# The bias of X's projection in a graph attention stage: from two VectorE additions a graph to one-row matmuls on TensorE, with the result copied out by ScalarE

## The reference, cut to what matters

```python
X = _heads(lrelu(node_feats @ W_lin + b_lin), B, N)      # lrelu(z) = leaky_relu(z, 0.01)
q = _heads(lrelu(node_feats @ W_q), B, N)
k = _heads(lrelu(node_feats @ W_k), B, N)
att = jax.nn.sigmoid(jnp.einsum('bhxd,bhyd->bhxy', q, k) * scale)
adj_h = adj_matrix[:, None] * att
deg = jnp.sum(adj_h, axis=-1)
dis = jnp.where(deg > 0, deg ** (-0.5), 0.0)
A = dis[..., :, None] * adj_h * dis[..., None, :]
Y = jnp.einsum('bhxy,bhyd->bhxd', A, X)
```

## Time and profile before

| | us |
|---|---|
| median of 3 runs (lowest to highest) | 1422.14 (1418.39 to 1423.32) |
| profiled execution | 1419.9 |
| span of its trace | 1418.2 |
| TensorE busy in the span | 1337.5 (94%) |
| VectorE busy | 962.3 (68%) |
| ScalarE busy | 794.9 (56%) |

### The profile page before, as it was taken

One profiled execution on the slowest core, in us unless ns is written; L12 is line 12 of the kernel. 1 busy time (PEld: TensorE's weight loads), 2 busy tenths in 40 slices (PEclk: granted clock), 3 DMA queues, 4 the chain that ended last, 5 costly groups with the idle time before them and its releaser, 6 DMA issues. The chain is left out here.

```text
span 1418.2 us, 27578 instructions
## 1 busy us (share of the span) xinstructions
PE 1337.5 (94%) x10184; PEld 806.0 (57%) x10184; DVE 962.3 (68%) x2147; ACT 794.9 (56%) x1334; POOL 581.7 (41%) x504
## 2 busy tenths in 40 slices
PE   5999999999999999986899999999999789999798
PEld 3455555668999999862233233333332467774498
DVE  2467887643343434357989999999996799856533
ACT  2466654644444444436676776777874578873300
POOL 2026777672545555301212132131143699972300
PEclk9999999999999999999999999999999999999999
DMA  9757757355888878555424534333331421004034
GB/s 312 274 178 251 288 161 236 118 179 149 248 252 240 253 242 252 173 153 178 142 90 135 162 102 126 93 118 108 102 105 45 117 61 46 16 1 98 1 107 134
DMA packets 200152, 214.37 MB, mean 151 GB/s; under 512 B 22949, under 2 KB 156645, under 8 KB 200020
## 3 DMA queue, kind: packets, MB, share of 16 engines
q1 hardware_dynamic: 191604, 195.24, 45.2%
q0 software_dynamic: 8416, 17.38, 3.4%
HBM read 170.51 MB, written 42.06 MB: 150 GB/s over the span
## 5 line engine op out<-in xcount | busy, mean ns | idle before, releaser
L1552 ACT ACTIVATE c_AH<-c_S 128x2048 f32<-128x2048 f32 x128 | 240.6, 1880 | 130.1 <-PE c_S L1417 129.8
L1586 DVE TENSOR_TENSOR c_AH<-c_AH,c_A 128x2048 f32<-128x2048 f32 x128 | 291.9, 2285 | 23.7 <-ACT c_AH L1552 16.3
L875 ACT ACTIVATE a_A<-a_DG,a_A 128x256 f32<-128x256 f32 (+2 forms) x202 | 94.8, 509 | 192.8 <-PE a_DG L728 191.7
L618 POOL DMA_INDIRECT ys<-a_A,a_targets x135 | 131.2, 972 | 142.3 <-DVE a_A L1090 123.8
L1375 POOL TENSOR_TENSOR c_raw<-c_deg,c_power 128x16 f32<-128x16 f32 x16 | 58.2, 3636 | 243.6 <-DVE c_deg L1643 243.6
L592 POOL DMA_INDIRECT rows<-a_S,a_slots x128 | 131.9, 1030 | 51.5 <-issue 51.5
L1444 PE MATMUL c_DG<-c_AH,c_ones 128*32 128x512 f32 x1024 | 137.3, 608 | 7.9 <-DVE c_AH L1586 7.9
L1417 PE MATMUL c_S<-c_Q,c_K 32*128 32x512 f32 x928 | 132.3, 640 | 5.1 <-ACT c_AH L1552 3.1
L1430 PE MATMUL c_YA<-c_AH,c_XT 128*32 128x512 f32 x1024 | 131.9, 593 | 0.3 <-DVE c_XT L1653 0.3
L698 PE MATMUL a_AG<-a_A,x 128*128 128x512 f32 x256 | 114.4, 595 | 0.0
L728 PE MATMUL a_DG<-a_A 128*128 128x256 f32 (+2 forms) x356 | 100.5, 406 | 1.2 <-DMA a_A<-xT_all 1.1
(11 more groups left out here) (428 smaller groups left out, 2497.7 us busy)
## 6 DMA issues: line engine op xcount, KB each, us to landing
a_A<-in_dram SPq DMA_DIRECT2D x76, 578.0 KB, 5.1
a_A<-in_dram SPq DMA_DIRECT2D x32, 1024.0 KB, 9.8
c_A<-in_dram SPq DMA_DIRECT2D x128, 256.0 KB, 2.6
a_A<-rows SPq DMA_DIRECT2D x60, 130.0 KB
G<-ys SPq DMA_DIRECT2D x10, 512.0 KB, 5.1
a_X<-in_dram SPq DMA_DIRECT2D x8, 512.0 KB, 13.4
a_R<-in_dram SPq DMA_DIRECT2D x8, 512.0 KB, 5.0
stream<-a_R SPq DMA_DIRECT2D x8, 512.0 KB, 9.7
```

The source lines that it names most:

```text
L618: pool.indirect_dma_start(ys, bass.IndirectOffsetOnAxis(ap=targets[g % NY][:, t:t + 1], axis=0), Y[g % NY][:, t, :], None, bounds_check=ys ...
L875: act.activation(hT[g % 2][:, f, 0:size(g)], up_bank(g, f)[:, 0:size(g)], ACT.Gelu, bias=w_of(g)[:, F_N + f:F_N + f + 1]).then_inc(h_ready, 1)
L1552: act.activation(AH[g % UNITS][:, :, :], S[:, :, :], ACT.Sigmoid, scale=HD ** -0.5).then_inc(att_ready, 1)
L1586: dve.tensor_tensor(ah[:, :, :], ah[:, :, :], A[g % ADJ_BUFS][:, :].unsqueeze(1).to_broadcast([P, HEADS, HALF]), ALU.mult).then_inc(ah_dve, 1)
```

## The change

`add_bias` and its two VectorE instructions a graph go. On TensorE each block of 128 nodes gets four more matmuls behind its four: the stationary operand is one row of 32 ones (`ones[0:1, :]`), the moving operand one row with the bias (`bias[0:1, :]`), and they accumulate onto the same four strips of `M`. On ScalarE a plain copy (`copy_X`) of `M` into `XR` stands behind the sigmoids of steps 6 and 7. The wait for the bias's load moves from VectorE to TensorE, that for the last graph's `XR` from VectorE to ScalarE.

```diff
                 elif what[:-1] == "x":
+                    if i == 0:
+                        pe.wait_ge(w_loaded, 48)
                     for c in range(*part):
                         for j in range(HEADS):
                             at = (4 * half + c) * P + j * HD
-                            mm = pe.matmul(M[quad(j), c * P:(c + 1) * P], xnT[:, at:at + HD], W[:, 2, :], start=True, stop=True)
+                            pe.matmul(M[quad(j), c * P:(c + 1) * P], xnT[:, at:at + HD], W[:, 2, :], start=True, stop=False)
+                        for j in range(HEADS):
+                            mm = pe.matmul(M[quad(j), c * P:(c + 1) * P], ones[0:1, :], bias[0:1, :], start=False, stop=True)
...
+            def copy_X(i, half):
+                act.wait_ge(side_full, full[f"x{half}", i])
+                wait(act, xs_ready, 2 * i)
+                act.activation(flat(XR[:, tiles(half), :]), M[:, :], ACT.Copy).then_inc(side_free, 1)
...
+                    if n in (6, 7) and is_graph(i):
+                        copy_X(i, n - 6)
...
-            def add_bias(i, half):
-                if i == 0:
-                    dve.wait_ge(w_loaded, 48)
-                dve.wait_ge(side_full, full[f"x{half}", i])
-                wait(dve, xs_ready, 2 * i)
-                dve.tensor_tensor(XR[:, tiles(half), :], quarter(M[:, :]), bias[:, :].unsqueeze(1).to_broadcast([P, 4, D]),
-                                  ALU.add).then_inc(side_free, 1)
...
-                    if n in (6, 7) and is_graph(i):
-                        add_bias(i, n - 6)
```

## The result

| | before | after |
|---|---|---|
| median of 4 runs (lowest to highest), us | 1421.59 (1418.39 to 1423.32) | 1453.21 (1448.08 to 1453.59) |
| profiled execution, us | 1419.9 | 1453.56 |
| span of its trace, us | 1418.2 | 1451.8 |

The changed kernel takes 1.0219 times as long, with a 95% interval of 1.0201 to 1.0236: 2.2% slower, 31.6 us between the medians. The forecast was 1452.0 us.

What follows compares the result with a forecast made beforehand. TensorE's list, without gaps from the second graph on, was taken to bound the attention stage. Seven graphs at 27.9 us, plus 3.3 for the first, less 0.5 for VectorE, gave +30.7 us: 1452 us, range 1440 to 1459.

Steps and rivals of the forecast that it cites:

- What bounds the kernel: Attention stage, second graph on: TensorE's list without idle time sets the 54.94 us period, VectorE does not.
- The streaming: TensorE's added bias matmuls: 0.218 us for each of 8 blocks, 1.74 us a graph, one contraction row no shorter than 128.
- The change of shape: TensorE alternating between 128*32 projection and 32*32 bias matmuls: 16 changes of 0.14 us, 2.24 us a graph.
- Rival B: TensorE switches from 128*32 to 32*32 at no price: 1.74 us a graph, period 56.7 us, 1435 us; chance 9%.
- The first graph: First graph of the stage: 3.98 us, less waits filled, plus half-clock cost, taken as 3.3 us, ends 0 to 5.0.
- the late half of C: ScalarE's copy makes the sigmoid late, TensorE idling before step 9's scores: 1457 us; C as a whole 7%.
- the waits of 0.51 and 0.22 us: First graph, steps 7 and 8: TensorE waits for ScalarE's sigmoid; added work can fall into these waits.
- the first job at half the clock: First graph, the job at 659 us: runs at granted clock 0.50 and may cost up to 1 us more.
- VectorE's gain: Eighth graph, step 10: losing the additions removes TensorE's 0.51 us wait for VectorE, a gain of 0.5 us.
- ScalarE: Copies in steps 6 and 7 stay off the path; the sigmoid of step 8 still waits 0.4 us for the scores.
- The sum: Whole kernel: 27.9 + 3.3 - 0.5 = +30.7 us, forecast 1452 us.

Runs made afterwards that it cites:

- experiment 1: Changed kernel without the one-row matmuls, so the bias is not added, ScalarE's copies kept: 1419.00 us against 1419.22 for the kernel before, ratio 0.9999.
- experiment 2: Changed kernel with VectorE instead of ScalarE copying M out at steps 6 and 7, one-row matmuls kept: 1451.78 us, ratio 1.0225 to the kernel before.
- experiment 7: Kernel before with VectorE's bias step split into an in-place addition and a separate copy out: 1421.53 us against 1419.95, ratio 1.0015.
- experiment 3: Changed kernel with bias matmuls of 128 contraction rows, in the projection's own array shape: 1432.33 us, ratio 1.0100 to the kernel before.
- experiment 6: Kernel of experiment 5 with its one-row matmul standing twice in each job, with ones of 0.5: 1455.73 us, ratio 1.0258 to the kernel before.
- experiment 4: Changed kernel with four 512-column one-row matmuls ahead of each job's projection, 4 shape changes a graph instead of 16: 1438.84 us, ratio 1.0139 to the kernel before.
- experiment 5: Changed kernel with one 512-column one-row matmul a job behind the scores, x0 whole behind step 6's degrees: 1438.73 us, ratio 1.0135 to the kernel before.

## Why the prediction was right, point by point

**What bounds the kernel: right.** TensorE's list set the period before (54.94 us), and does after. Experiments 1, 2 and 7 show it from three sides.

**The streaming: right.** 1.74 us a graph forecast, 1.75 measured (experiment 3). That one contraction row is as dear as 128 was read from the scores and the degrees, and holds: 512 columns of one row take 0.85 us (experiment 6), `x1`'s 512 columns of 128 rows 0.87.

**The change of shape: right, a little too high.** 0.14 us a change was taken from a block between two other shapes; experiments 3 and 4 give 0.135 and 0.13. For 16 changes that is 2.16 instead of 2.24 us, and the graph 3.91 instead of 3.98. Rival B, a period of 56.7 us, is the kernel of experiment 3 and not this one. So going from 128\*32 to 32\*32, with the column strips unchanged, pays like the pairs seen before. The Trainium skill's rule that a change of tiling mode drains TensorE ("TensorEngine Tiling (Array Packing)", "Tiling Modes") now has a price for this pair too, 0.13 to 0.135 us; the drain itself no row shows.

**The first graph: too low.** 3.3 us forecast, with 5.0 as the upper end; 4.6 measured. The rows of TensorE's first graph after, answering to the earlier trace rows:

```profile
658.69 1.93 PE L1444 MATMUL c_DG<-c_AH,c_ones 128*32 128x512 f32 x8 [4.99 <-DVE c_AH L1597]
660.40 0.66 PE L1479 MATMUL c_M<-W,xnT 128*32 128x128 f32 x8
...
662.73 2.09 PE L1417 MATMUL c_S<-carry,c_K 32*128 32x512 f32 x8
664.75 1.57 PE L1444 MATMUL c_DG<-c_AH,c_ones 128*32 128x512 f32 x8
666.15 0.39 PE L1479 MATMUL c_M<-W,xnT 128*32 128x128 f32 x8
...
667.53 1.14 PE L1417 MATMUL c_S<-carry,c_K 32*128 32x512 f32 x8
...
672.29 1.14 PE L1417 MATMUL c_S<-c_Q,carry 32*128 32x512 f32 x8
...
675.98 1.14 PE L1417 MATMUL c_S<-c_Q,carry 32*128 32x512 f32 x8 [0.97 <-ACT c_AH L1561]
```

From the first projection (660.40) on, the distances between it and the scores are 2.33, 4.80, 4.76 and 3.69 us; between the starts in the earlier trace rows (659.12, 660.13, 664.22, 667.45, 670.58) they are 1.01, 4.09, 3.23 and 3.13. The differences, 1.32, 0.71, 1.53 and 0.56, make 4.12; the other 0.5 us lies ahead of that, in steps that the change does not touch. Two things of it were not in my sum. The waits of 0.51 and 0.22 us were filled as forecast, but the one of 0.41 grew to 0.97: ScalarE's copy and normalisations stand ahead of the sigmoid, and in the first graph no products cover them. In experiment 2, without that copy, the row reads

```profile
672.99 1.14 PE L1417 MATMUL c_S<-c_Q,carry 32*128 32x512 f32 x8 [0.42 <-ACT c_AH L1561]
```

Idle time ahead of the scores of step 9 is the sign that the prediction gave for the late half of C; it has grown in the first graph alone.

And the clock stays down longer. After, the granted clock by stretches reads

```profile
662.00:664.00 2.00, 2.00 (x21) 0.71 (x16) 1.12 (x1) 0.00 (x0) 0.00 (x0) 0.50 1.11 330
664.00:666.00 2.00, 2.00 (x12) 0.40 (x12) 0.00 (x0) 1.11 (x1) 0.00 (x0) 0.54 0.79 278
```

It rises at about 666 us, 7 us after the degrees that end the idle time, where before it rose at 662.3, 5 us after them:

```profile
657.41 1.93 PE L1444 MATMUL c_DG<-c_AH,c_ones 128*32 128x512 f32 x8 [4.79 <-DVE c_AH L1586]
```

I had priced only the first job at half the clock; the degrees behind the next scores (1.40 us to the next start) ran at it as well. Why it rose later is open. In the first graph the clock stood at 0.50 for 10.2 us here and in the experiments 2, 4 and 5, and for 13.7 us in experiment 6, all with one-row matmuls; before, and in the experiments 1, 3 and 7, which have none, for 6.8 us in all. That is one trace of each kernel, and no run tested the cause. In experiment 3 the first graph was 1.5 us longer than before from its first projection on, and 0.4 us in all, because its earlier waits were 1.0 us shorter. Experiment 2 does not show that the copy alone costs 0.56 us in all: its clock rose later still, and its first graph was as long as this one's.

**VectorE's gain: right.** 0.5 us forecast; the wait of 0.51 us in the eighth graph is gone, and that graph grew by 3.3 instead of 3.9 us.

**ScalarE: right.** 0.4 us of cover forecast at step 8, 0.32 measured.

**The sum.** +30.7 us forecast, 31.4 in the stage and 31.6 between the medians. The changes of shape were booked some 0.5 us too dear over seven graphs, the first graph 1.3 too cheap: that the total is closer than its terms is luck.

The step that did fail is one of an experiment: the 0.43 us in the expectation of number 5. I took the time that a block needs for four strips together and divided where nothing is to be divided: one strip with 512 columns is as long as four.

## What to carry to other kernels

Before moving work from a busy engine, find the one whose list has no gaps from period to period: 11 us taken from an engine that is 88 to 97% busy were worth 0.5 us, and 3.9 us a graph added to the one without gaps were paid in full. In these runs a bias row on TensorE cost its columns whatever the contraction, and a change of array shape on each side: if it must be there, give it the shape of its neighbours (here 1.75 instead of 3.91 us a graph), or group it. Price a tiled matmul by the columns of its longest strip, not by its share of the array.

## What the runs showed of the hardware

- A change between 128\*32 and 1\*32 matmuls costs 0.13 to 0.135 us although both have 32-column strips; it appears in no row as idle time.
- An fp32 matmul with one contraction row and 512 columns that sits in one strip alone takes 0.84 to 0.86 us, as long as four side by side.
- A stretch with two such matmuls in a row was followed, in two graphs of seven (the fifth and the eighth), by some 3 us at a granted clock of 0.50, with TensorE busy throughout (experiment 6). With one of them (experiment 5) the period was the same in all later graphs. What decides it was not tested.
